# Second pass of the norms in a graph layer: GpSimd takes the scaling and one tile of each group

## The reference

```python
            y = x + core                       # core: the output of the experts
            mean = jnp.mean(y, axis=0)
            var = jnp.mean((y - mean) ** 2, axis=0)
            return (y - mean) * jax.lax.rsqrt(var + BN_EPS) * gamma + beta
...
    x = _layernorm(x + _L0_gnn_ref(x, ...), axis=-1)   # (z - mean) / sqrt(var + 1e-5) over the 256 features
```

## Time and profile before

| what | us |
|---|---|
| median of three runs | 3444.21 |
| profiled execution, its own time | 3441.13 |
| its span | 3439.4 |
| VectorE busy over the span | 1966.5 (57%) |
| ScalarE busy over the span | 1186.2 (34%) |
| GpSimd busy over the span | 2143.5 (62%) |
| from the first `times_scale` (3343.27) to the end of the span | 96.1 |

### The profile page before, as it was taken

One profiled execution on the slowest core, in us unless ns is written; L12 is line 12 of the kernel. 1 busy time (PEld: TensorE's weight loads), 2 busy tenths in 40 slices (PEclk: granted clock), 3 DMA queues, 4 the chain that ended last, 5 costly groups with the idle time before them and its releaser, 6 DMA issues. The chain is left out here.

```text
span 3439.4 us, 60389 instructions
## 1 busy us (share of the span) xinstructions
PE 2788.5 (81%) x15009; PEld 2009.6 (58%) x15146; DVE 1966.5 (57%) x6832; ACT 1186.2 (34%) x2847; POOL 2143.5 (62%) x2204
## 2 busy tenths in 40 slices
PE   3664888888888888888888888868999999999650
PEld 3543544444455555555555555538899889888540
DVE  6993444444455555555555555555555555555598
ACT  2992222222222222222222222224444444444239
POOL 4576777777777777777777777734555555545300
PEclk8886999999999999999999999989999999999885
DMA  8867444444444444444444444434544544444477
GB/s 344 328 182 237 132 129 129 128 129 128 128 146 135 137 136 134 149 134 136 135 148 136 135 137 135 136 113 128 157 139 146 168 139 130 152 149 132 140 269 245
DMA packets 275801, 539.24 MB, mean 157 GB/s; under 512 B 46441, under 2 KB 184014, under 8 KB 271296
## 3 DMA queue, kind: packets, MB, share of 16 engines
q0 software_dynamic: 102912, 274.26, 28.0%
q1 hardware_dynamic: 169904, 224.40, 19.4%
q10 hardware_dynamic: 2832, 38.69, 2.7%
HBM read 413.04 MB, written 128.92 MB: 158 GB/s over the span
## 5 line engine op out<-in xcount | busy, mean ns | idle before, releaser
L1307 POOL DMA_INDIRECT work<-h_table,src_cols x1570 | 1488.0, 948 | 493.9 <-issue 467.0
L1685 PE MATMUL ps<-work 128*128 128x257 f32 x3322 | 1072.3, 405 | 274.9 <-DMA work<-h_table,src_cols 251.0
L1685 PEld LDWEIGHTS ps<-work 128*128 128x128 f32 x3322 | 554.0, 190 | 712.2 <-issue 495.0
L1327 DVE TENSOR_TENSOR work<-rel_cols,ps 128x1152 f32<-128x1152 f32 x196 | 251.1, 1282 | 878.2 <-PE ps L1685 878.1
L1558 PE MATMUL ps<-none_w,none 128*128 128x512 bf16 x1257 | 478.5, 381 | 0.0
L1824 POOL DMA_INDIRECT picked<-ys,places x232 | 249.2, 1074 | 364.2 <-DVE ys L1894 344.5
L1941 PEld LDWEIGHTS ps<-xst,work 128*128 128x128 f32 x3648 | 443.2, 192 | 27.9 <-issue 15.9
L1941 PE MATMUL ps<-xst,work 128*128 128x128 f32 x3648 | 447.0, 276 | 10.6 <-issue 9.9
L1948 PE MATMUL ps<-work,hid 128*128 128x256 f32 x1824 | 436.0, 382 | 1.7
L1805 ACT ACTIVATE hid<-ps,b_cols 128x128 f32<-128x128 f32 x912 | 315.7, 367 | 169.2 <-PE ps L1941 126.4
L1948 PEld LDWEIGHTS ps<-work,hid 128*128 128x128 f32 x1824 | 328.6, 190 | 47.2 <-ACT hid L1805 11.7
(11 more groups left out here) (297 smaller groups left out, 3837.5 us busy)
## 6 DMA issues: line engine op xcount, KB each, us to landing
work<-in_L_gnn_w_dram SPq DMA_DIRECT2D x128, 512.0 KB, 4.7
work<-h_table,src_cols POOLq DMA_INDIRECT x1570, 2.8
picked<-acc ACTq DMA_DIRECT2D x1, 25088.0 KB, 114.3
pk<-picked SPq DMA_DIRECT2D x13, 1792.0 KB, 10.5
m_base<-acc ACTq DMA_DIRECT2D x1, 12642.0 KB, 37.3
acc<-m_base SPq DMA_DIRECT2D x14, 903.0 KB, 6.1
x_beta<-xr_x SPq DMA_DIRECT2D x98, 128.0 KB, 1.9
pk<-x_beta SPq DMA_DIRECT2D x14, 896.0 KB, 6.2
```

The source lines that it names most:

```text
L1307: pool.indirect_dma_start(out=got[:, c % RING, 0:D], out_offset=None, in_=h_table[:, :], in_offset=bass.IndirectOffsetOnAxis(ap=src_cols[: ...
L1327: nc.vector.tensor_tensor(hot[:, (2 * t + h) % HOTS, 0:b - a, :], rel_cols[:, a:b].unsqueeze(2).broadcast_to([P, b - a, P]), lanes.unsquee ...
L1685: mm = nc.tensor.matmul(ps_flat[:, bank(t, k, w[0])], hot[:, (2 * t + (k >= HALF)) % HOTS, k % HALF if k >= HALF else k, :], got[:, c % RI ...
```

## The change

`times_scale` goes from VectorE to a new GpSimd block, which scales groups 0 and 1 and then, for each g, group g+2, and normalises the last tile (`ON_POOL` = 1) of each group but the last. ScalarE squares 4 tiles instead of 5 and normalises 6 instead of 7; VectorE squares 3 instead of 2. The counts of `normed` follow, and the store and ScalarE's root also wait for `normed_by_pool`.

```diff
--- before.py
+++ after.py
@@ -1965,7 +1965,8 @@
         GT = 7
         NG = NT // GT
         B = 4
-        ON_ACT = 5
+        ON_ACT = 4
+        ON_POOL = 1
         LAST_ON_ACT = 4
         FIRST_PARTS = ((0, 2), (2, 4), (4, GT))
         LAST_PARTS = ((0, 3), (3, 5), (5, GT))
@@ -2011,6 +2012,7 @@
         shift_set = sem2("shift_set")
         normed = sem2("normed")
         normed_by_dve = sem2("normed_by_dve")
+        normed_by_pool = sem2("normed_by_pool")
 
         def group(g, a=0, b=GT):
             return acc3[:, g * GT + a:g * GT + b, 0:D]
@@ -2050,7 +2052,8 @@
 
                 def store(g):
                     if g < NG - 1:
-                        sp.wait_ge(normed, GT * (g + 1))
+                        sp.wait_ge(normed, (GT - ON_POOL) * (g + 1))
+                        sp.wait_ge(normed_by_pool, g + 1)
                         sp.dma_start(out[g * GT * P:(g + 1) * GT * P, :].rearrange("(t p) d -> p t d", p=P),
                                      pk[:, held(g), :, 0:D]).then_inc(o_out[held(g)], 16)
                         return
@@ -2058,7 +2061,7 @@
                     sp.dma_start(out[(g * GT + LAST_ON_ACT) * P:(NT - 1) * P, :].rearrange("(t p) d -> p t d", p=P),
                                  pk[:, held(g), LAST_ON_ACT:GT - 1, 0:D]).then_inc(o_out[held(g)], 16)
                     sp.dma_start(out[(NT - 1) * P:N, :], pk[0:LAST, held(g), GT - 1, 0:D]).then_inc(o_out[held(g)], 16)
-                    sp.wait_ge(normed, GT * g + LAST_ON_ACT)
+                    sp.wait_ge(normed, (GT - ON_POOL) * g + LAST_ON_ACT)
                     sp.dma_start(out[g * GT * P:(g * GT + LAST_ON_ACT) * P, :].rearrange("(t p) d -> p t d", p=P),
                                  pk[:, held(g), 0:LAST_ON_ACT, 0:D]).then_inc(o_out[held(g)], 16)
 
@@ -2120,13 +2123,6 @@
                 dve.wait_ge(gamma_in, 16)
                 dve.wait_ge(scale_part, 1)
                 nc.vector.tensor_tensor(scale[:, :], scale[:, :], gamma_b[:, :], ALU.mult).then_inc(scale_set, 1)
-                dve.wait_ge(scale_set, 1)
-                dve.wait_ge(centred, NG - 1 + len(LAST_PARTS))
-
-                def times_scale(g):
-                    nc.vector.tensor_tensor(group(g), group(g), scale[:, :].unsqueeze(1).broadcast_to([P, GT, D]),
-                                            ALU.mult).then_inc(scaled, 1)
-
                 def residual(g):
                     dve.wait_ge(scaled, g + 1)
                     dve.wait_ge(xb_in[held(g)], 16 * (g // B + 1))
@@ -2160,7 +2156,6 @@
                     nc.vector.tensor_tensor(shift[:, g % 2, :], z_mean[:, g % 2, :], rstd[:, g % 2, :], ALU.mult).then_inc(shift_set, 1)
 
                 for g in range(NG):
-                    times_scale(g)
                     if g > 0:
                         spreads(g - 1)
                     residual(g)
@@ -2176,6 +2171,29 @@
                     nc.vector.tensor_scalar(pk[:, held(g), u, 0:D], tile(g, u), rstd[:, g % 2, u:u + 1], shift[:, g % 2, u:u + 1],
                                             ALU.mult, ALU.add).then_inc(normed_by_dve, 1)
 
+            @block.gpsimd
+            def _(pool):
+                pool.wait_ge(scale_set, 1)
+                pool.wait_ge(centred, NG - 1 + len(LAST_PARTS))
+
+                def times_scale(g):
+                    nc.gpsimd.tensor_tensor(group(g), group(g), scale[:, :].unsqueeze(1).broadcast_to([P, GT, D]),
+                                            ALU.mult).then_inc(scaled, 1)
+
+                def normalise(g):
+                    pool.wait_ge(shift_set, g + 1)
+                    for u in range(GT - ON_POOL, GT):
+                        last = nc.gpsimd.tensor_scalar(pk[:, held(g), u, 0:D], tile(g, u), rstd[:, g % 2, u:u + 1], shift[:, g % 2, u:u + 1],
+                                                       ALU.mult, ALU.add)
+                    last.then_inc(normed_by_pool, 1)
+
+                for g in range(2):
+                    times_scale(g)
+                for g in range(NG - 1):
+                    if g + 2 < NG:
+                        times_scale(g + 2)
+                    normalise(g)
+
             @block.scalar
             def _(act):
                 for g in range(NG):
@@ -2199,12 +2217,13 @@
                 def root(g):
                     act.wait_ge(spread_set, g + 1)
                     if g >= 2:
-                        act.wait_ge(normed, GT * (g - 1))
+                        act.wait_ge(normed, (GT - ON_POOL) * (g - 1))
+                        act.wait_ge(normed_by_pool, g - 1)
                     nc.scalar.activation(rstd[:, g % 2, :], spread[:, g % 2, :], ACT.Sqrt).then_inc(spread_rooted, 1)
 
                 def normalise(g):
                     act.wait_ge(shift_set, g + 1)
-                    for u in range(LAST_ON_ACT if g == NG - 1 else GT):
+                    for u in range(LAST_ON_ACT if g == NG - 1 else GT - ON_POOL):
                         nc.scalar.activation(pk[:, held(g), u, 0:D], tile(g, u), ACT.Identity, bias=shift[:, g % 2, u:u + 1],
                                              scale=rstd[:, g % 2, u:u + 1]).then_inc(normed, 1)
 
```

## The result

The changed kernel takes 3469.87 us (median of 4 runs, 3468.83 to 3473.43) against 3443.45 before: a ratio of 1.0078, 95% interval 1.0062 to 1.0094, or 26.4 us slower. The forecast was 3479, slower, in a range of 3440 to 3494: the direction and the mechanism held, the size was too large by a third.

The account below looks back on a forecast made before the run. ScalarE's chain was taken to bound the second norm pass, 6.04 us a group. After: 56.0 + 6.0 + 60.9 - 3.5 = 119.4 against 82.9 us, +36.5, less 1.0 at the end: +35.5, 3479 us, range 3440 to 3494.

Parts of the forecast that it names:

- Whether the engines run side by side: Second norm pass: GpSimd's product and VectorE's two-SBUF-input instructions exclude each other for whole instructions, so times add; chance 0.68.
- The length of the product: GpSimd's 128x1792 scaling product per group: 4.0 us, between 2.9 and 4.2; 14 products make 56.0 us.
- the float32 row: VectorE's 128x1274 float32 comparison, 0.23 us lost beside a 98-column GpSimd subtraction; by columns a product of 4.2 us.
- the bf16 rows: VectorE's bf16 pair, 0.15 to 0.18 us lost beside GpSimd; by columns, from 0.16, a product of 2.9 us.
- The normalisation: GpSimd's 128x256 normalisation per group: 0.7 us, of which 0.5 on the common path; 12 make 6.0 us.
- What may hide under the product: VectorE's one-input mean, reciprocal and spreads, 7 us in all, may run under GpSimd instructions; half, 3.5 us, given back.
- VectorE's own time: Second norm pass: 4.06 us per group today, 4.47 with a third square; 60.9 us to the last `minus_mean`.
- the stretch up to the last `minus_mean`: From 3343.27 us in the second norm pass: 82.9 us today, 119.4 forecast, 36.5 more.
- ScalarE's saving: One square and one normalisation less: 1.0 us a group, hidden while ScalarE idles; -1.0 us behind the last `minus_mean`.
- The added waits: GpSimd's wait for `shift_set`, ScalarE's root and SP's store waiting for GpSimd's tile: cost nothing under exclusion.
- What would show it: A VectorE residual held about 4 us, products 8 to 9 us apart, ScalarE waiting 3.5 us a group for `z_mean`.

Follow-up runs that it names:

- The scaling alone: Changed kernel with only the scaling on GpSimd, still paced, and the normalisation back on ScalarE: 3462.22 us against 3438.97 for the kernel before.
- the missing spreads: Changed kernel without VectorE's spreads instruction, ScalarE taking the root from dev directly: ratio 1.0073 to the kernel before, +24.7 us.
- the PSUM operand: Changed kernel without spreads, second operand of VectorE's residuals and squares from PSUM, part of the computation left out: pass 85.3 us, group 5.11.
- the unpaced run: Kernel with only the scaling on GpSimd, its waits for each group's shift removed, 14 products in a row: 3489.31 us against 3446.7 before.
- a version faster than before: Against the kernel before: scaling on VectorE, no spreads, 7 squares on ScalarE, 3 normalisations on GpSimd: 3434.26 against 3437.18 us, ratio 0.9988.

## Why the prediction was right, and where its size was off

- **Whether the engines run side by side.** Right, from 1x98 instructions to one of 3.8 us. The scaling alone, the missing spreads and the PSUM operand each show it in another instruction.
- **The length of the product.** I chose 4.0 us between 2.9 and 4.2, by the float32 row. The part that excludes VectorE is 3.43 to 3.45; the other 0.35 us of the recorded 3.80 is not exclusive. By columns 3.43 us is 0.19 us for 98, between the 0.16 and 0.23 that I scaled from, so the scaling over a factor of 18 in columns held. 14 x 0.57 = 8.0 us too much. This is the term that failed most: the bf16 rows bounded it from below and I gave them too little weight.
- **The normalisation.** 0.5 us on the common path; measured 0.12 on the square beside it (0.61 instead of 0.48), since GpSimd does most of the waiting. 12 x 0.38 = 4.6 us too much.
- **What may hide under the product.** I gave back 3.5 us for VectorE's small one-input instructions. They are held as well: spreads, the one that met the product, lost 2.8 us, and in the unpaced run the mean took 3.54. 3.5 too little. The three together are -9.1 of the -10.1 by which the stretch up to the last `minus_mean` was off (119.4 forecast, 109.3 measured).
- **VectorE's own time.** The last 1.0 us comes mostly from here. The 4.06 us that I took from the earlier trace rows as VectorE's work held 0.19 us of waiting for ScalarE's root: the mean and the reciprocal start 0.27 us apart there, and 0.08 in the changed kernel (the two lines below). 13 x 0.19 = 2.5 us too much. Against it stand +1.3 in the two groups that have no product beside them, where VectorE waits for ScalarE's squares (5.04 us from mean to mean instead of 4.40), and +0.3 in the first product, which VectorE waits for from end to end (3.74 us). The steady group then adds up: 4.06 - 0.19 + 0.41 + 0.12 + 3.43 = 7.83, measured 7.81.

```profile
3371.47 0.17 DVE L2136 TENSOR_SCALAR z_mean<-z_sum 128x7 f32<-128x7 f32 x1
3371.55 0.19 DVE L2154 RECIPROCAL rstd<-rstd 128x7 f32<-128x7 f32 x1
```

- **ScalarE's saving.** Hidden, as written: it waits 44.7 us for `z_mean`, 15.8 of them at the head and 2.4 in a steady group, where I had named 3.5. Behind the last `minus_mean` the pass is 12.3 us instead of 13.2, -0.9 for the -1.0 forecast.
- **The added waits.** GpSimd's wait for `shift_set` proved a help: with the scaling alone on GpSimd the pass is 119.4 us with it and 140.4 without.
- **What would show it.** I had named a residual of about 4 us in the steady part. It is there only at the head. Later the product starts behind the shift and GpSimd's normalisation, during VectorE's third square (3372.98), and the next instruction in VectorE's order is spreads; with spreads removed it is the residual, 3.84 us. Spreads comes 0.57 us later than it could, since it waits for ScalarE's fourth square, so its recorded hold is 2.8 us and not 3.4. Products start 7.8 us apart, under the 8 to 9 that I named; my own terms give a group of 4.47 + 4.0 + 0.5 - 0.25 = 8.7, where I wrote 8.6.

## What to carry to other kernels

Work moved from VectorE to GpSimd can come back as standing still: here a product of 2.0 us on VectorE cost it 3.4 us, because the product reads SBUF and VectorE's residuals and squares take two inputs from it. What counts is what the moved instruction costs its neighbour, not whether GpSimd has time: the 128x256 normalisation reads SBUF too, but costs VectorE only 0.12 to 0.25 us, and three of them a group were part of a version faster than before. Before moving work, look for short GpSimd instructions anywhere in the trace that lie beside VectorE instructions with two SBUF inputs; if they end when VectorE's do, expect the lengths to add, as they did here. A tiny instruction with a mean of microseconds, or "issue" in the chain where an engine had work, is the sign of it afterwards.

## What the runs showed that I had not expected

- The turn changes after each instruction even when VectorE has a queue: when the last of 14 unpaced products was done (3400.5, 53 us after the first began), VectorE had finished its first group and was ending the third residual of the second.
- Small one-input VectorE instructions are held by GpSimd instructions that only write (mean 0.63 us, spreads 2.25, instead of 0.17), while residuals with two inputs are not, unless they queue behind a held one.
- GpSimd's 128x256 normalisation is cheap for VectorE (0.12 to 0.20 us each, and 0.25 on the first residual behind VectorE's product with three of them, 3370.63 to 3371.23) even where it takes 0.97 us itself.
